# Spreading the FFN jobs of a gated recurrent layer thinner over the attention chunks, and moving two elementwise steps from VectorE to ScalarE and GpSimd

## The reference, cut to what matters

```python
xn = layernorm(x)
# attention: a linear recurrence with decay, per head
q, k, v = xn @ Wq, xn @ Wk, xn @ Wv ; q, k = rope(q), rope(k)
beta = clip(sigmoid(xn @ Wg + bg), 0.8, 0.9995)
phi_q, phi_k = elu(q) + 1, elu(k) + 1
S = S * b_t + phi_k (outer) v ;  z = z * b_t + phi_k      # step by step over t
y_t = (phi_q S) / (phi_q . z + 1e-6)
s = y @ Wo + bo
# FFN, integer weights with zero point 128 and a scale per output row (hidden width 5632)
g = silu( (silu(xn @ Wgate.T) * (xn @ Wup.T)) @ Wdown.T )
out = x + s * g
```

## Time and profile before

| | us |
|---|---|
| median of 2 runs | 4828.7 (4827.1 to 4830.2) |
| the profiled execution | 4811.8 |
| its span on the slowest core (core 6) | 4810.2 |
| spans of the 8 cores | 4750.5 to 4810.2 |
| TensorE busy, core 6 | 3185.4 |
| VectorE busy | 1042.5 |
| ScalarE busy | 465.8 |
| GpSimd busy | 538.4 |
| the stage of the change, first scores to last chunk | about 1517 to 3481 |

### The profile page before, as it was taken

How to read it: one execution, slowest core, us unless ns; L and a number is a source line. 1 busy time by engine, 2 the same in 40 slices (tenths; PEclk the granted TensorE clock), 3 DMA queues, 4 the chain that set the end, 5 groups by cost and what they waited for, 6 DMA issues and landing times.

```text
span 4810.2 us, 43668 instructions; the slowest of 8 cores (4750.5 to 4810.2 us)
## 1 busy us (share of the span) xinstructions
PE 3185.4 (66%) x14783; PEld 1489.4 (31%) x15056; DVE 1042.5 (22%) x1854; ACT 465.8 (10%) x869; POOL 538.4 (11%) x633
## 2 busy tenths in 40 slices
PE   0004677777770699999998998833426888538888
PEld 0001333333330344444443443333302333213333
DVE  1233434343431121121111111232300000000000
ACT  0110122222220000110000000110100000000000
POOL 0101233333330000000000000000010000100000
PEclk9997799999985799999999999955567999769889
DMA  6663123232319654646544435452194444754443
GB/s 150 161 170 58 30 67 59 66 57 67 59 48 166 146 121 106 129 108 143 117 106 107 92 80 103 112 141 66 37 173 108 120 115 127 141 121 126 113 117 96
DMA packets 697785, 508.54 MB, mean 106 GB/s; under 512 B 426976, under 2 KB 629728, under 8 KB 691424
## 3 DMA queue, kind: packets, MB, share of 16 engines
q0 software_dynamic: 69360, 181.49, 17.9%
q1 hardware_dynamic: 458736, 162.73, 17.0%
q10 hardware_dynamic: 169472, 161.52, 12.6%
HBM read 337.83 MB, written 176.16 MB: 107 GB/s over the span
## 4 chain that ended last, share of the span: by engine, by line
PE 51%; DMA 14%; DVE 12%; SPq 7%; issue 6%; POOL 6%; ACT 2%; ACTq 1%; DVEq 1%; POOLq 0%
PE pb L710 13%; PE pb L718 12%; PE pb L1016 10%; SPq L962 6%; PE pb L941 5%; PE pb L570 4%; POOL swp L602 3%; DMA raws<-wqg 3%; DMA yTm<-yt_sp 2%; PE pb L831 2%; DMA xb<-x 2%; DMA raws<-wqu 2%; DMA vch<-v_sp 2%; DVE tmp L616 2%; DVE tmp L608 2%
## 5 line engine op out<-in xcount | busy, mean ns | idle before, releaser
L570 PE MATMUL pb<-ws,xnT 128*128 128x512 bf16 x2823 | 660.1, 392 | 122.1 <-DVE tmp L597 118.7
L710 PE MATMUL pb<-xnT,wgT 128*128 128x512 bf16 x2736 | 682.2, 403 | 32.6 <-DMA wgT<-wg_sp 26.4
L718 PE MATMUL pb<-xnT,wuT 128*128 128x512 bf16 x2762 | 635.7, 380 | 26.9 <-DMA wuT<-wu_sp 24.0
L1016 PE MATMUL pb<-wdT,guTm 128*128 128x512 bf16 x2417 | 531.6, 379 | 2.5
L570 PEld LDWEIGHTS pb<-ws,xnT 128*128 128x128 bf16 x2880 | 284.2, 100 | 496.7 <-issue 191.0
L710 PEld LDWEIGHTS pb<-xnT,wgT 128*128 128x128 bf16 x2816 | 279.0, 103 | 368.4 <-issue 103.3
L941 PE MATMUL pb<-wos,yTm 128*128 128x512 bf16 x939 | 267.5, 451 | 183.8 <-DMA yTm<-yt_sp 182.0
L718 PEld LDWEIGHTS pb<-xnT,wuT 128*128 128x128 bf16 x2816 | 276.1, 98 | 358.3 <-issue 27.6
L723 DVE SCALAR_TENSOR_TENSOR gub<-pb,gsb 128x512 bf16<-128x512 f32 x176 | 121.6, 691 | 1131.2 <-PE pb L718 369.1
L1016 PEld LDWEIGHTS pb<-wdT,guTm 128*128 128x128 bf16 x2464 | 241.2, 98 | 290.6
L467 PE MATMUL pb<-xnT,wgb 128*16 128x512 bf16 x64 | 18.9, 462 | 400.6 <-DMA xnT<-xn_sp 386.6
(11 more groups left out here) (105 smaller groups left out, 2047.4 us busy)
## 6 DMA issues: line engine op xcount, KB each, us to landing
guTm<-gu_sp ACTq DMA_DIRECT2D x64, 704.0 KB, 9.1
raws<-wqg POOLq DMA_DIRECT2D x11, 2048.0 KB, 21.0
wg_sp<-raws POOLq DMA_DIRECT2D x11, 2048.0 KB, 10.7
raws<-wqu POOLq DMA_DIRECT2D x11, 2048.0 KB, 15.1
wu_sp<-raws POOLq DMA_DIRECT2D x11, 2048.0 KB, 10.4
gu_sp<-gub ACTq DMA_DIRECT2D x176, 128.0 KB, 2.3
raws<-wqd POOLq DMA_DIRECT2D x16, 1408.0 KB, 14.7
wd_sp<-raws POOLq DMA_DIRECT2D x16, 1408.0 KB, 8.1
```

The lines of the kernel that those rows point to most:

```text
L570: P.mm_group([(lambda e, k=k, m=m, sl=sl, pbank=pbank: e.matmul(pb[pbank][:, 0:512], xnT[:, k * L + m * 128:k * L + (m + 1) * 128], wslot[ ...
L710: P.mm_group([(lambda e, k=k, t=t, tb=tb, sl=sl: e.matmul(pb[6][:, 0:512], wgT[sl][:, k * FS + t * 128:k * FS + (t + 1) * 128], xnT[:, k * ...
L718: P.mm_group([(lambda e, k=k, t=t, tb=tb, sl=sl: e.matmul(pb[7][:, 0:512], wuT[sl][:, k * FS + t * 128:k * FS + (t + 1) * 128], xnT[:, k * ...
L1016: e.matmul(pb[pbank][:, 0:DDS], guTm[msl][:, kh * 256 + mi * 128:kh * 256 + (mi + 1) * 128], wdT[j][:, kh * DDS:(kh + 1) * DDS], start=(kh ...
```

## The change

Three edits, all inside the stage of interleaved attention and FFN:

- `emit_ffn` is called at three places of a chunk and no longer at five: the calls after the denominators and after the `sel4` matmuls are removed, and the last one puts 1 job, no longer 1 or 2 in turn. A chunk has 3 jobs, so the 176 jobs last for chunks 0 to 57 and 2 jobs of chunk 58.
- In every second job (the 2nd, 4th, ...: the counter is raised before it is tested) VectorE's multiply is replaced by two instructions: ScalarE copies bank 7 to a new bf16 buffer `upsb`, and GpSimd multiplies `upsb` with `gsb` into `gub`. The store of `gub` on ScalarE's queue then waits for GpSimd.
- The copy of the transposed reciprocals to `rrow` moves from VectorE to ScalarE.

```diff
+            upsb = [sb(f"upsb{i}", [128, 512], BF16, stack=s3) for i in range(2)]
...
-                    P.op("ve", lambda e, ii=ii: e.scalar_tensor_tensor(
-                        out=gub[ii][:], in0=pb[7][:, 0:512], scalar=1.0, in1=gsb[ii][:],
-                        op0=ALU.mult, op1=ALU.mult),
-                        reads=[pbB[7], gsbB[ii]], writes=[gubB[ii]])
+                    if cur["ffn"] % 2 == 0:
+                        P.op("se", lambda e, ii=ii: e.activation(upsb[ii][:], pb[7][:, 0:512],
+                                                                AF.Copy),
+                             reads=[pbB[7]], writes=[upsbB[ii]])
+                        P.op("ge", lambda e, ii=ii: e.tensor_tensor(
+                            gub[ii][:], upsb[ii][:], gsb[ii][:], ALU.mult),
+                            reads=[upsbB[ii], gsbB[ii]], writes=[gubB[ii]])
+                    else:
+                        P.op("ve", ...
...
                     P.mm_group(den_fns, reads=[stbB, qTgB, AmB[cp], constsB], writes=[pbB[2]])
-                    emit_ffn(1)
...
-                    P.op("ve", lambda e, rrow_=rrow_: e.tensor_copy(rrow_[:], pb[3][0:HG, 0:128]),
+                    P.op("se", lambda e, rrow_=rrow_: e.activation(rrow_[:], pb[3][0:HG, 0:128],
+                                                                   AF.Copy),
...
-                    emit_ffn(1)
                     P.op("se", lambda e, nsb_=nsb_, bkN=bkN: e.activation(
...
-                    emit_ffn(1 + (c % 2))
+                    emit_ffn(1)
```

More of the change, by code:

```diff
@@ L673, in build_program @@
             gubB = P.bufs("gub", 2)
+            upsbB = P.bufs("upsb", 2)
             nft = FS // 128
@@ L722, in emit_ffn @@
                         reads=[wuTB[sl], xnT_half_tok(tb * 512)], writes=[pbB[7]])
-                    P.op("ve", lambda e, ii=ii: e.scalar_tensor_tensor(
-                        out=gub[ii][:], in0=pb[7][:, 0:512], scalar=1.0, in1=gsb[ii][:],
-                        op0=ALU.mult, op1=ALU.mult),
-                        reads=[pbB[7], gsbB[ii]], writes=[gubB[ii]])
+                    if cur["ffn"] % 2 == 0:
[6 more added lines that the diff above has]
+                    else:
+                        P.op("ve", lambda e, ii=ii: e.scalar_tensor_tensor(
+                            out=gub[ii][:], in0=pb[7][:, 0:512], scalar=1.0, in1=gsb[ii][:],
+                            op0=ALU.mult, op1=ALU.mult),
+                            reads=[pbB[7], gsbB[ii]], writes=[gubB[ii]])
                     P.dma("se", lambda e, ht=ht, tb=tb, ii=ii: e.dma_start(
```

## The result

| | us |
|---|---|
| median of the changed kernel (11 runs) | 5059.5 |
| ratio to the kernel before, from runs next to each other | 1.047, 95% interval 1.0428 to 1.0512 |
| the same on 4828.7 us | +227, interval +207 to +247 |
| profiled execution, its span (core 6) | 5024.0, 5022.4 |
| predicted | 5145, range 4960 to 5270 (+316.5) |

Slower, as forecast, and inside the range; the loss is about 90 us smaller than forecast. Some executions of most of these kernels, four of the 11 here, are longer while the cores of one die show a lower granted clock than the others; every ratio in this text leaves them out (the median of the other seven is 5052.1 us).

The account below looks back on a forecast made before the run. TensorE was taken as the bound; jobs, attention matmuls, waits, clock and bare chunks summed to 2173.6 us against 1843.3, less 13.8 in chunk 0: +316.5 on 4828.7, 5145 us, range 4960 to 5270.

Parts of the forecast that it names:

- The new wait: Even chunks 2 to 54: load issued behind GpSimd's multiply, so the numerator waits 15.8 us (gate, up) or 13.8 us (down).
- T0: The moment when TensorE is done with the last job of an odd chunk; the forecast counts its times from it.
- The other waits: TensorE's waits before transpose and fp32 matmuls: 0.70 and 1.95 us in even chunks, 1.35 and 0.5 in odd ones.
- preparation waits: Numerator waits at 27 weight preparations in even chunks 2 to 54: 11 x 15.8 + 16 x 13.8 = 394.6 us.
- group starts: Chunks 16, 32 and 48: `kTg` and preparation loads share one wait, plus 5 us each for contention, 15 us.
- clock: TensorE clock loss: 3.2 us in 29 odd chunks, 2.0 in 29 even ones, more after long waits; 215.6 us.
- short waits: TensorE's small waits in chunks 1 to 58: 29 x (2.65 + 1.85) + 3.4 = 133.9 us.
- landing: Time for a preparation's weight load to arrive: taken as 16 us, from earlier medians of 15.4 and 14.7 us.
- cheap wait: Rival, 0.14: the wait exists, but landings are at their minima and clock loss is 120; +155, 4984 us.
- the 250: Upper clock loss in us, if every burst behind a wait for data starts at the lower clock.
- covered case: Rival, 0.07: loads are early enough and chunks are covered; -71.5, 4757 us, or 4728 with clock losses as now.
- long clock loss: Rival, 0.06: TensorE falls to 1.2 GHz much longer, one more half-speed gate in 58 chunks, 200 us; 5345 us.

Follow-up runs that it names:

- earlier load: Changed kernel with the next weight preparation's load issued one chunk earlier, at the odd chunk ahead of its multiplies; 0.988 of the kernel before.
- other half: Changed kernel with the 1st, 3rd, 5th ... jobs split instead of the 2nd, 4th ...; 0.9883 of the kernel before.
- held-back load without arithmetic: Kernel before with three jobs per chunk, all on VectorE, plus the preparation's load waiting for `gub` of the previous chunk's last job; 1.0462 of the kernel before.
- thin kernel: Kernel before with three jobs per chunk alone, all multiplies and `rrow` on VectorE; 0.9867 of the kernel before.
- last two versions: Covered kernel with `vch`, `hch` loaded a chunk ahead: 0.9222; that plus two jobs at each group's end and `qTg`/`kTg` issued behind its last denominators: 0.9204.
- covered one: Kernel before with three VectorE jobs per chunk, one in each gap, VectorE's small attention step issued before each job; 0.9329 of the kernel before.
- last version: Covered kernel with `vch`, `hch` loaded a chunk ahead, two more jobs at each group's end, `qTg`/`kTg` issued behind its last denominators; 0.9204 of the kernel before.

## Why the prediction was right, and where its size was off

Right, by its own steps:

- *The new wait.* The order alone said that the load would go out behind the last job. Read at T0 + 2.4, measured T0 + 2.3; the multiply 1.27, measured 1.15. TensorE idles before the numerator in even chunks, ended by `Am`, VectorE waiting for `raws` in all 27. Three experiments show this as the cause (earlier load, other half, held-back load without arithmetic). One sign of its own did not hold: it named idle times of 12 to 18 us, and the 14 down blocks have 8.8 to 11.1.
- *The other waits.* 1.95 in even chunks and 0.5 in odd ones before the fp32 matmuls, 0.7 and 1.3 before the transpose: read 1.9 to 2.0 and 0.5; 60.8 and 73.7 us in sum. The wait before the numerator in odd chunks is gone. The price of `rrow` behind ScalarE's DMA issue is the 40.2 us above.
- *Chunk 0:* -13.8, measured -15.0. *Clock of the stretch:* about 0.85, measured 0.85, although the term that it stands for was half as large again as the measured one, as the table shows.

The forecast stretch was 2173.6 us, the measured one 2059.5: 114 too much, in two terms, with a third against them.

| term | predicted | measured | off |
|---|---|---|---|
| preparation waits, 24 chunks | 10 x 15.8 + 14 x 13.8 = 351.2 | 294.2 | -57 |
| the 3 group starts with theirs | 15.8 + 2 x 13.8 + 15 = 58.4 | about 75 | +17 |
| clock | 215.6 | about 143 | -72 |
| short waits | 133.9 | about 131 | -2 |

(The waits of chunks 1 to 58 are 294.2 + 75 + 131, about 501. The clock is what is left of 2059.5 after them and after 1195.4 of jobs, 164.7 of attention matmuls and 54.4 of bare chunks. The 75 are the 69.9 for `kTg` and 1.9 in each of the three chunks.)

- *Preparation waits.* Gate and up blocks came as forecast: 14.3 to 16.6 us, mean 15.3 against 15.8. Down blocks took 8.8 to 11.1, mean 10.1 against 13.8. The step that failed is the landing: "part of the time SyncE's transposing loads run beside it, ..., so I take 16", for both kinds. The landing in this trace is 10.5 to 17.2 with a median of 12.8 (gate and up blocks 15.2, down blocks 12.1), where the earlier trace rows has 12.6 to 23.5. What differs is what stands ahead of the load: before it was the store of the last block, half a microsecond earlier on the same queue, now it is a multiply. Landings of the 16 down blocks in the change, in the kernel with the earlier load and in the thin kernel, where the load still follows the store:

```profile
DMA to landing us min/median/max: 10.5/12.1/14.0
DMA to landing us min/median/max: 11.0/12.1/15.3
DMA to landing us min/median/max: 12.7/14.5/41.6
```

  A busier DMA does not explain it: the second and the third kernel both have a DMA share of 0.50 in chunks 1 to 63. The same split runs through all traces. On the profiled core the shortest landing of a down block is 10.0 to 11.3 us in the six kernels whose load does not follow the store, and 12.6 to 14.0 in the seven where it does. No run moved the store alone.
- *A slip in the sum.* 2.4 + 16 + 1.7 + 1.5 is 21.6 and not 20.95, so a down block's wait was 14.45 by its own terms, and the sum 10 us more. The bound of 328 us at the shortest landings was worked out with 14.45; with 13.8 it is 317, and the cheap wait would be +143 instead of +155.
- *Clock.* "I take a loss of 3.2 us in all 29 odd chunks" failed. Odd chunks last 25.2 to 27.2 us without their waits for `vch` and `kTg`, and that leaves 0 to 1.8 us of loss, 1.2 on average; 29 x 2.0 is 57 of the 72 us, and the even chunks have the other 15. In odd chunks the fp32 matmuls still run at full speed (1.12 us), and in 23 of the 29 the drop comes later, in the gate: 5.30 us in chunk 7, but 3.61 in chunk 1, where there is none. In the earlier trace rows it had come before the fp32 matmuls. The Trainium skill ("TensorE: Matmul & The Clock Gate", HAM oscillation) describes a kernel in which every burst behind a wait for data starts at the lower clock; the trace agrees behind the long waits (6.09 us for a gate) and not right behind the short gaps of odd chunks. Taken for every gap, as I did for the 250, it would have been further off than my 215.6.
- *Group starts.* The three waits for `kTg` are 22.9, 19.6 and 27.4 us, and the numerator then waits only 1.9: they share one wait with the preparation, as forecast, but it is longer than the preparation's by more than the 5 us I gave it.

The rivals: the covered case failed as its own text said (the order decides). Its 4757 us come close to the kernel with the early load, 0.988 or 4771 us, but by luck: the stretch of that trace is 1856.7 us where its sum has 1785.6, above all with 86.9 us at `kTg` for its 40.5 and the 74 at `vch`. The cheap wait, +155, had the right direction of error: landings near their minimum and a clock term of about 120 were both half true. The long clock loss did not occur.

The Trainium skill's reason against the split was that VectorE was not saturated ("Perfetto Trace Analysis", Optimizing Scalar/DVE Operations). The runs agree that there was nothing to win: with the load early, the split kernel (0.988) and the one without it (0.9867) cannot be told apart. But by that reason it would have been free, and where it stood it turned the thin kernel's 0.9867 into 1.0334 (with `rrow` on VectorE in both).

## What to carry to other kernels

Before an instruction is put on another engine, read what stands behind it in that engine's stream, DMA issues first: GpSimd was idle for nine tenths of this stage, and three short multiplies in front of a load, with one small copy behind a DMA issue, turned a gain of 1.3% into a loss of 4.7%. A job that is to cover a gap helps only if the small step that the gap waits for is issued ahead of that job's own evacuation on the same engine; here that was worth 5% beyond the thinning. And an issue that is moved to cover one transfer has to be followed through the queue of every transfer that it triggers: what is next on SyncE can be 32 loads.

## What the runs showed of the hardware that was not expected

- Four transposing loads of `kTg` on one queue took from 11.9 us (chunk 16, above) to 38.3 us (chunk 48), and in the thin kernel 48.7 us at chunk 32, by SyncE's timeline:

```profile
2547.04 48.72 SPq L754 DMA_TRANSPOSE kTg<-kt_sp  x4
```

  Single ones lasted 2.0 to 26.3 us there. Each of the slowest coincides with a weight preparation: in the thin kernel at chunk 32 and in the last two versions at chunk 48 a `kTg` load took 43.1, 53.0 and 34.8 us to land, and about 1 us behind it GpSimd issued the store of a down block and the next load, which landed after 27 to 45 and 34 to 52 us, where others nearby took about 6 and 13 to 14. All three transfers are slow together; which one holds up which was not tried. By this, much of what is left at the group starts is not SyncE's order.
- GpSimd's multiply of two bf16 inputs of 128x512 took 1150 ns, against 1270 and 1483 for the rows of f32 inputs and about 690 ns for VectorE's, which reads one input as f32 from PSUM: a factor of 1.7. The Trainium skill ("GPSIMD Engine Reference", 4.1 Engine selection) gives about 2 for two inputs; the trace is somewhat better.
- The granted clock of chunks 1 to 63 followed the gaps and not the amount of TensorE's work, which is the same in these kernels: 0.85 in the change, 0.89 in the thin kernel, 0.94 in the covered one, and in the last version, whose window shows it with 1474.3 us for chunks 1 to 63, 0.96:

```profile
1627.60:3101.90 1474.30, 1375.60 (x7872) 689.97 (x7868) 392.36 (x801) 181.44 (x300) 32.70 (x53) 0.96 0.64 132
```
